# Graph attention on one core: the upper half of the adjacency moved to Pool's DMA queue, and ScalarE's q factors and the eighth score matmul moved ahead

## The reference

```
s_i = x @ attn[:128];  s_j = x @ attn[128:]
e = leaky_relu(s_i + s_j.T, 0.2) + where(adj > 0, 0, -1e9)
y = x + softmax(e, axis=1) @ x
out = (y - mean(y)) / sqrt(var(y) + 1e-5)
```

## Time and profile before

| | us |
|---|---|
| median of 3 runs | 273.63 (273.01 to 275.97) |
| the profiled execution | 275.48, of which its span 273.7 |

### The profile page before, as it was taken

The page is one execution under the profiler, slowest core; times in us unless marked ns, Lnnn a source line. Parts: engine busy times, 40 slices in busy tenths (PEclk is TensorE's granted clock), DMA queues, the critical chain, the costliest instruction groups (busy, mean ns, idle before and its releaser), DMA issues.

```text
span 273.7 us, 5248 instructions
## 1 busy us (share of the span) xinstructions
PE 250.0 (91%) x2113; PEld 244.2 (89%) x2113; DVE 237.8 (87%) x377; ACT 168.7 (62%) x239; POOL 35.7 (13%) x74
## 2 busy tenths in 40 slices
PE   4694991999999999999999999999999999999970
PEld 4553991999999999999999999999999999999970
DVE  0779934899999999999999999999999999999251
ACT  0578157976769759874996199519960898044010
POOL 3000000000015003300330033003300330033010
PEclk9797797799999999999999999999999999999996
DMA  6999999999999999999999999999999510001001
GB/s 168 305 348 348 333 224 331 349 347 349 349 348 349 359 349 347 354 357 349 348 334 353 350 310 279 356 348 291 257 349 349 167 42 1 2 0 41 0 1 44
DMA packets 70427, 71.75 MB, mean 262 GB/s; under 512 B 2992, under 2 KB 68912, under 8 KB 70400
## 3 DMA queue, kind: packets, MB, share of 16 engines
q1 hardware_dynamic: 34816, 34.80, 42.1%
q10 hardware_dynamic: 34624, 34.67, 41.7%
q0 software_dynamic: 960, 1.90, 2.4%
HBM read 69.27 MB, written 2.10 MB: 261 GB/s over the span
## 4 chain that ended last, share of the span: by engine, by line
PE 83%; DMA 5%; ACTq 5%; DVE 3%; ACT 1%; issue 1%; DVEq 0%
PE psum L717 83%; DMA adj_in<-in_adj_dram 5%; ACTq L233 3%; ACTq L219 2%; DVE mask_bytes L522 1%; DVE weights L609 1%; ACT mask_bytes L368 0%; ACT L368 0%; DVE mask_t L517 0%; DVE xj L527 0%; PE psum L702 0%; ACT q_row L348 0%; ACT q_row L354 0%; DVE x_raw L586 0%; DVE x_raw L554 0%
## 5 line engine op out<-in xcount | busy, mean ns | idle before, releaser
L717 PEld LDWEIGHTS psum<-xj,weights 128*128 128x128 f32 x2048 | 233.7, 195 | 11.3 <-DVE weights L609 6.0
L717 PE MATMUL psum<-xj,weights 128*128 128x129 f32 x2048 | 234.0, 278 | 9.8 <-DVE weights L609 9.8
L609 DVE SCALAR_TENSOR_TENSOR weights<-q_row,r_j,mask_t 128x512 f32<-128x512 f32 x256 | 172.8, 740 | 2.5
L368 ACT ACTIVATE mask_bytes<-adj_in,sig_bias 128x4096 uint8<-128x4096 int32 x30 | 110.5, 3700 | 19.0 <-issue 16.5
L517 DVE STREAM_TRANSPOSE mask_t<-mask_bytes 128x1024 uint32<-128x1024 uint32 x32 | 39.6, 1237 | 9.6 <-ACT mask_bytes L368 9.5
L376 ACT ACTIVATE x_raw<-x_raw 128x128 f32<-128x128 f32 x28 | 8.3, 298 | 34.1 <-DVE x_raw L554 30.0
L299 POOL TENSOR_SCALAR neg_mean<-total 128x4 f32<-128x4 f32 x7 | 3.0, 422 | 180.9 <-ACT x_raw L376 180.9
L308 POOL DMA_DIRECT2D out_dram<-x_raw x28 | 14.5, 521 | 20.6 <-ACT x_raw L390 20.5
L383 ACT ACTIVATE unused<-x_raw,neg_mean 128x128 f32<-128x128 f32 x28 | 10.9, 390 | 3.9 <-POOL neg_mean L299 3.9
L390 ACT ACTIVATE x_raw<-x_raw,offset,rstd 128x128 f32<-128x128 f32 x28 | 11.5, 479 | 2.3 <-POOL offset L305 2.3
L489 DVE TENSOR_TENSOR adj_in<-x_raw,attn_j 128x1024 f32<-128x1024 f32 x4 | 4.8, 1221 | 8.5 <-DMA attn_j<-in_L_gnn_attn_dram 8.2
(11 more groups left out here) (55 smaller groups left out, 55.9 us busy)
## 6 DMA issues: line engine op xcount, KB each, us to landing
adj_in<-in_adj_dram SPq DMA_DIRECT2D x64, 512.0 KB, 13.4
adj_in<-in_adj_dram ACTq DMA_DIRECT2D x64, 512.0 KB, 15.6
out_dram<-x_raw POOLq DMA_DIRECT2D x28, 64.0 KB, 5.4
x_raw<-in_x_dram ACTq DMA_DIRECT2D x8, 128.0 KB, 6.1
x_raw<-in_x_dram SPq DMA_DIRECT2D x8, 128.0 KB, 5.3
out_dram<-x_raw SPq DMA_DIRECT2D x4, 32.0 KB, 1.6
attn_j<-in_L_gnn_attn_dram POOLq DMA_DIRECT2D x1, 64.0 KB, 6.9
out_dram<-x_raw ACTq DMA_DIRECT2D x4, 16.0 KB, 1.6
```

The lines of the kernel that those rows point to most:

```text
L368: nc.scalar.activation(mask_bytes[:, g % BYTE_SLOTS, :, :, :], adj_in[:, g % ADJ_SLOTS, :, :, :], ACT.Sigmoid, bias=sig_bias[:], scale=200 ...
L609: nc.vector.scalar_tensor_tensor(weights[:, slot_of(n, c), :], q_row[:, n * BANK:(n + 1) * BANK], r_j[:, c:c + 1], mask_t[:, (n * PIECES + ...
L717: return nc.tensor.matmul(banks[(n * K + t) % 8][:, 0:D1], weights[:, slot_of(n, c), t * P:(t + 1) * P], xj[:, c, 0:D1], start=(c == 0), s ...
```

## The change

- Pool's queue, not ScalarE's, issues the high half of every piece of the adjacency. It starts when the third stripe of x has landed, issues pieces 0 to 6 under the same conditions as SP, and from then on piece g + 5 when piece g has been converted. The statistics and stores of a block are put between these issues, at the places at which ScalarE's order reaches them.
- Each half of a slot has its own semaphore; the conversions wait for both.
- ScalarE issues only its part of x. Its relus run in the order 0, 3, 1, 2, 4, 5, 6, 7 (the exponential of the first part behind relu 0), then the large exponential, then `scale_xj(1)`, then the conversions.
- TensorE runs the eighth score matmul before all products; it waits for relu 3, now the second. The first product waits for four relus where it waited for three.

```diff
-    S_I_LATE_AT = 5
+    S_I_ORDER = [0, 3, 1, 2, 4, 5, 6, 7]
...
             for g in range(ALL_PIECES):
-                load_piece(sp, LOW_HALF, g)
+                load_piece(sp, LOW_HALF, g, adj_low_loaded)
...
+            pool.wait_ge(x_loaded[STRIPES - 2], 16 * Q)
+            for g in range(ADJ_SLOTS + BY_DVE):
+                load_piece(pool, HIGH_HALF, g, adj_high_loaded)
+            for g in range(BY_DVE, ALL_PIECES):
+                if g + ADJ_SLOTS < ALL_PIECES:
+                    load_piece(pool, HIGH_HALF, g + ADJ_SLOTS, adj_high_loaded)
+                if g % PIECES == PIECES - 1 and g > PIECES:
+                    row_statistics(g // PIECES - 1)
+                if g % PIECES == 0 and g > PIECES:
+                    store_block(g // PIECES - 2)
+            store_block(NORM_GROUPS - 1)
...
             for st in range(STRIPES):
                 load_x(act, HIGH_HALF, st)
-            load_piece(act, HIGH_HALF, 0)
             for m in range(RB):
                 act.wait_ge(xT_in_psum, m + 1)
                 nc.scalar.copy(xT[:, m * BANK:(m + 1) * BANK], banks[XT_BANK + m % 4][:, :]).then_inc(xT_ready, 1)
-                if m in (1, 5):
-                    load_piece(act, HIGH_HALF, 1 + m // 4)
...
-                act.wait_ge(adj_loaded[g % ADJ_SLOTS], 16 * Q * (g // ADJ_SLOTS + 1))
+                act.wait_ge(adj_low_loaded[g % ADJ_SLOTS], 16 * len(LOW_HALF) * (g // ADJ_SLOTS + 1))
+                act.wait_ge(adj_high_loaded[g % ADJ_SLOTS], 16 * len(HIGH_HALF) * (g // ADJ_SLOTS + 1))
...
-                if g - 1 + ADJ_SLOTS < ALL_PIECES:
-                    load_piece(act, HIGH_HALF, g - 1 + ADJ_SLOTS)
...
             q_factors(0, 1)
-            s_i_piece(1)
-            s_i_piece(2)
-            scale_xj(1)
-            load_piece(act, HIGH_HALF, PROD_SLOT)
-            for rb in range(3, RB):
+            for rb in S_I_ORDER[1:]:
                 s_i_piece(rb)
             q_factors(1, RB)
-            load_piece(act, HIGH_HALF, XT_SLOT)
-            load_piece(act, HIGH_HALF, ADJ_SLOTS)
+            scale_xj(1)
...
-                    pe.wait_ge(s_i_ready, S_I_BANK.index(bank) + 1)
+                    pe.wait_ge(s_i_ready, S_I_ORDER.index(S_I_BANK.index(bank)) + 1)
...
-            for rb in range(4, RB - 1):
+            for rb in range(4, RB):
                 s_i_piece(rb)
...
-                    if n == 0 and c == S_I_LATE_AT:
-                        s_i_piece(RB - 1)
...
-                            pe.wait_ge(s_i_ready, 3)
+                            pe.wait_ge(s_i_ready, 4)
```

More of the change, by code:

```diff
@@ L140, in gat_kernel @@
         attn_loaded = sem("attn_loaded")
-        adj_loaded = [sem(f"adj_loaded{i}") for i in range(ADJ_SLOTS)]
+        adj_low_loaded = [sem(f"adj_low_loaded{i}") for i in range(ADJ_SLOTS)]
+        adj_high_loaded = [sem(f"adj_high_loaded{i}") for i in range(ADJ_SLOTS)]
         stored = sem("stored")
@@ L220, in load_x, with load_piece @@
                                 x_v[q, :, st * SC // K:(st + 1) * SC // K, :]).then_inc(x_loaded[st], 16)
-        def load_piece(queue, quadrants, g):
+        def load_piece(queue, quadrants, g, loaded):
             if g == PROD_SLOT:
@@ L233, in load_piece @@
                 queue.dma_start(adj_in[B * q:B * (q + 1), g % ADJ_SLOTS, :, :, :],
-                                adj_v[g // PIECES, g % PIECES, q, :, :, :, :]).then_inc(adj_loaded[g % ADJ_SLOTS], 16)
+                                adj_v[g // PIECES, g % PIECES, q, :, :, :, :]).then_inc(loaded[g % ADJ_SLOTS], 16)
         def store_last(queue, g, q):
@@ L294, in _, with row_statistics, store_block @@
             nc.gpsimd.memset(worst[:], 0.0).then_inc(worst_ready, 1)
-            for g in range(NORM_GROUPS):
-                pool.wait_ge(total_ready, g + 1)
+            def row_statistics(n):
+                pool.wait_ge(total_ready, n + 1)
                 nc.gpsimd.tensor_scalar(neg_mean[:, 0:K], total[:, 0:K], -1.0 / D, 0.0, ALU.mult, ALU.add).then_inc(mean_ready, 1)
-                pool.wait_ge(squares_ready, g + 1)
+                pool.wait_ge(squares_ready, n + 1)
                 nc.gpsimd.tensor_scalar(variance[:, 0:K], square_sum[:, 0:K], 1.0 / D, EPS, ALU.mult, ALU.add).then_inc(variance_ready, 1)
-                pool.wait_ge(variance_ready, g + 1)
+                pool.wait_ge(variance_ready, n + 1)
                 nc.gpsimd.tensor_tensor(rstd[:, 0:K], variance[:, 0:K], half[:, 0:K], ALU.pow).then_inc(rstd_ready, 1)
-                pool.wait_ge(rstd_ready, g + 1)
+                pool.wait_ge(rstd_ready, n + 1)
                 nc.gpsimd.tensor_tensor(offset[:, 0:K], neg_mean[:, 0:K], rstd[:, 0:K], ALU.mult).then_inc(offset_ready, 1)
-                pool.wait_ge(out_ready, g + 1)
+            def store_block(n):
+                pool.wait_ge(out_ready, n + 1)
                 for q in range(Q):
-                    pool.dma_start(out_v[g, q, :, :],
-                                   x_raw[B * q:B * (q + 1), g * K:(g + 1) * K, :].rearrange("b k d -> b (k d)")).then_inc(stored, 16)
+                    pool.dma_start(out_v[n, q, :, :],
+                                   x_raw[B * q:B * (q + 1), n * K:(n + 1) * K, :].rearrange("b k d -> b (k d)")).then_inc(stored, 16)
+            pool.wait_ge(x_loaded[STRIPES - 2], 16 * Q)
[9 more added lines that the diff above has]
+            store_block(NORM_GROUPS - 1)
             for g, v in enumerate(FINAL_GROUPS[:EARLY]):
@@ L519, in first_to_bytes @@
             def first_to_bytes(g):
-                dve.wait_ge(adj_loaded[g], 16 * Q)
+                dve.wait_ge(adj_low_loaded[g], 16 * len(LOW_HALF))
+                dve.wait_ge(adj_high_loaded[g], 16 * len(HIGH_HALF))
                 nc.vector.tensor_scalar(mask_bytes[:, g, :, :, :], adj_in[:, g, :, :, :], 0.0, None,
```

## The result

The changed kernel takes 335.58 us (median of 4, 334.24 to 337.01) against 273.4 us beside it: a ratio of 1.2245, 95% interval 1.2196 to 1.2293. It is slower by 62 us. The forecast was 267.1 us, 264.5 to 271.3.

The account below looks back on a forecast made before the run. It took the first 51 us, before TensorE's unbroken products, as the bound: -5.85 (gap) -1.97 (half clock) -0.69 (matmul) +2.0 (piece 0 later) = -6.5 us, so 267.1 us, with 264.5 to 271.3 for 8 in 10.

Parts of the forecast that it names:

- What bounds the kernel now: TensorE's products run unbroken at full clock for the last 218 us, so only the first 51 us can move the end.
- the gap: TensorE's idle time from 41.10 to 46.95 before the fifteenth weight; claimed to go altogether, 5.85 us.
- the half clock behind it: 18 TensorE records after the gap took 3.99 us where 2.02 would do; claimed gain 1.97 us.
- the matmul in between: Eighth score matmul between TensorE's products, 32.21 to 32.90; moving it into idle time was to gain 0.69 us.
- first stretch at half clock: TensorE at half clock from 24.77 to 30.46; claimed to stay, since TensorE is idle before its first product in both kernels.
- ScalarE's new order: Reordered ScalarE work and table load were to end at 31.7, `scale_xj(1)` at 30.4, so the transfer decides piece 2.
- What Pool pays for an issue: Each of Pool's 64 DMA issues was to take 0.7 to 1.7 us, hidden behind everything; upper bound 8.1 us.
- the rival R1: Pool's descriptor issues become the bound, over 3.6 us each; at 4.0 us each the kernel takes 292 us; chance 0.14.
- the term of +2.0 us: Start of piece 0's conversion on VectorE shifts later to 21.2 us, by +2.0, bounds -0.5 to +5.5.
- at 349 GB/s a piece takes 6.0 us: Adjacency transfer rate per piece, set against 7.2 us of products and 6.6 us of VectorE work.
- each further piece has more slack than the one before: After piece 2, with 1.7 us to spare, later pieces were to gain slack, at 6.0 us transfer against 7.2 of products.
- The forecast's list of signs: Error signs in the changed profile: Pool issues over 3.6 us, VectorE waiting for bytes behind 40 us, first conversion after 24 us.

Follow-up runs that it names:

- e5_act_late: `e1_order_only` with ScalarE's DMA issues moved behind the conversions; 266.31 us against 274.13, ratio 0.9729.
- e1_order_only: The kernel before with only ScalarE's new order and the eighth score matmul ahead of the products, loads still on ScalarE's queue; 273.35 us against 274.02, ratio 0.9987.
- m1_queues: A kernel that only loads adjacency quadrants, in eight stages of different queues, halves and run sizes, without attention; ran once, rates only, no time or ratio given.
- stage 7: Part of `m1_queues`: Pool's queue alone loads the high half in runs of 1 KB; as fast on a half as SP, limit 206 to 210 GB/s.
- stage 2: Part of `m1_queues`: SP loads the low half and Pool the high half, both in runs of 1 KB; 264 GB/s in sum.
- e7_pool_sp4k: The changed kernel with SP's low half loaded in runs of 4 KB, output no longer the layer's; 279.74 us, ratio 1.0148.
- e8_hw_sp4k: `e5_act_late` with SP's low half loaded in runs of 4 KB, no load on Pool's queue; 338.07 us, ratio 1.2282.
- stages 2 and 4: Parts of `m1_queues`: SP low with Pool high in 1 KB runs; SP low in 4 KB runs with ScalarE high in 1 KB; 264 GB/s in both.

## Why the prediction was wrong

**What bounds the kernel now: right.** The end was set by the first 51 us. `e5_act_late` takes away the gap, the half clock behind it and the matmul in between, which the sum put at 8.5 us, and gains 7.8 (274.13 - 266.31). That the two agree so well is in part luck. In the traces its products run from 23.54 to 255.24 us, 231.7 us, and before from 24.77 to 265.37, 240.6: 8.9 us less. About 1.1 us of that is a shorter first stretch at half clock, which ends at about 27.2 us instead of 30.46 and which the prediction had staying; and the products start 1.2 us earlier, which the sum did not have.

**ScalarE's new order: right.** Its work ended even 1.5 us earlier than worked out (28.9 against 30.4); 1.2 us of that is VectorE's `below_max`, which it waits for and which started at 17.31 instead of 18.51. The prediction counted on the issues being gone from ScalarE, and `e1_order_only` shows that the whole gain hangs on that.

**What Pool pays for an issue: right.** From 0.7 to 1.7 us was taken; 64 issues took 705 to 1122 ns, median 740:

```profile
L234 POOL DMA_DIRECT2D adj_in<-in_adj_dram x64: 705/740/1122, 10.8 to 272.7; - x64
```

The estimate from the count of runs (0.74 us) met the median. So the rival R1, which forecast a loss, has the sign and not the mechanism: Pool had time enough and was idle three quarters of the span.

**Piece 0: the term of +2.0 us was mis-sized.** Its conversion starts at 24.52, a shift of 5.3, close to the high end of 5.5. Pool issued at 10.78, 0.9 us before the 11.7 of the sum, but up to 18.0 us q0 moved nothing, while q1 moved 0.91 MB from 12.8 to 17.6 us alone. So the first bytes took 7.2 us, where the sum had 3.6 for the whole latency and 5.3 at most, and the move took 6.5 us (5.9 in the sum). In `m1_queues` Pool's first bytes came about 1.4 us after the issue in stage 7, with no other queue at work, and 3.1 us in stage 2, where SP's queue started with it; that they are late because SP's queue is already full fits these three, but no run tests it alone. The bounds of the shift held; the middle was too hopeful. This alone would have cost 3.3 us of the gain.

**The step that failed is the rate.** "at 349 GB/s a piece takes 6.0 us" was carried over from the kernel before into one in which one of the two queues is of another kind, and with it the step that "each further piece has more slack than the one before". That the share of a queue could be uneven stood in the working, but only as a gain for piece 0 (4.8 us instead of 6.0); what the other queue loses by it was not put down, nor that the sum falls with it. With the measured rates the time comes out. While Pool's half of a piece moves, 1.05 MB at 206 GB/s (6.99 MB in 34 us), 5.1 us pass, in which SP's half gets 1.90/34 of 5.1 us, 0.28 MB. The other 0.77 MB move alone at 191: 4.0 us. That is 9.1 us for a piece (230 GB/s), where TensorE uses one up in 7.2 us (291 GB/s); 32 of them are 291 us, and with a start near 11 us the loads end at about 302; the slices say 299. The products, VectorE's end of the last block and the stores come behind that, and the span is 332.4. This sum was made with the rates measured in the changed kernel; that its two causes are real rests on `m1_queues`, `e7_pool_sp4k` and `e8_hw_sp4k`.

**What could have been seen.** Both numbers stood in the kernel before. One half of the partitions alone reached 217 GB/s; it was used as a rate that Pool's queue might enjoy, not as a ceiling that makes two even shares necessary. And the list of queues of the profile's page before gives Pool's 1.90 MB in 960 packets beside 34.80 MB in 34816, 2.0 KB against 1.0 KB, which asks what a packet is on each. The forecast's list of signs had a first conversion later than 24 us and VectorE waiting for bytes behind 40 us as signs of error; both appeared.

## What to carry to other kernels

Before a load moves to another queue, compare the packet sizes of all queues that will be full together: here they took turns packet by packet, so the bytes went as the packet sizes, and the consumer waited for the half that got less. Keep the two halves of the partitions in use at once and evenly. If DMA issues hold an engine up, first try putting them right behind a long instruction of that engine, before looking for another queue: that was worth 2.7% here.

## What the hardware showed that I had not expected

- Two queues with packets of 1 KB and 4 KB took turns one to one, so bytes went 3.6 or 3.7 to 1, whichever of the queues had the large ones (stages 2 and 4 of `m1_queues`, and `e8_hw_sp4k`).
- Quadrants 0 and 1 together took 209 GB/s, quadrants 0 and 2 took 347, from the same two queues.
- The sum of two queues of 4 KB packets on different halves was 289 GB/s, below the 347 of two with 1 KB. This is not explained.
- Pool's queue moved nothing for about 7 us after its first issue, while SP's queue was full; with no other queue at work it was about 1.4 us (stage 7 of `m1_queues`).
